# The expert's second bias as a one-row product on TensorE in 22 of 77 visits

## The chip, the cores and the metric

The kernel runs on one core of one Trainium2 chip. The metric is the device time of one execution in microseconds (us). Engines are named as in the profile: PE is TensorE's matmul, PEld its weight load, DVE is VectorE, ACT is ScalarE, POOL is GpSimd and SP is SyncE, which here only starts transfers.

## The reference, cut to what matters

One layer on 32 batches of 256 rows of 128 numbers (8,192 rows): modulated layernorm, attention with 16 heads, a residual sum, and then a mixture of 14 experts of which each row uses one. The change concerns the last part alone:

```python
hid = jnp.einsum('nd,edf->nef', x, w1) + b1          # 128 -> 256
hid = jax.nn.gelu(hid, approximate=False)
all_out = jnp.einsum('nef,efd->ned', hid, w2) + b2   # 256 -> 128, b2: one row of 128 per expert
sel = jnp.take_along_axis(all_out, assignments[:, None, None], axis=1)[:, 0, :]
moe_out = (sel * weights[:, None]).reshape(Bb, Ss, Dd)
...
x = x + gb * moe_out
```

All of it is fp32. `b2` is drawn with a spread of 2, so it matters to the output.

## The kernel before, in words

**Attention stage, 0 to about 491 us.** One batch is one iteration. TensorE makes scores, ScalarE their exponentials, VectorE the row maxima, GpSimd the normalisation and the scatter of finished rows into a table in device memory, sorted by expert. In `project_out` (L1123 to L1133) TensorE already adds a bias by a product of 3 rows (`ones_s` and `bias_rows`, bf16, L1131) ahead of a full one of 128 rows (`w_gated`, fp32, L1132).

**Expert stage, about 491 us to the end.** The table is worked off in NT = 77 *visits* of 128 rows, each with one expert. All engines run the same order of visits, written out by hand; nothing is scheduled by costs. `over_tiles` counts a step j; in step j

- SP has loaded the rows of visit j (`load`, L729 to L746), into one of 21 rooms (16 in `x_s`, 5 in `more_rooms`);
- TensorE (`tile`, L1267) turns visit j (`turn_tile`, L1244: one instruction), makes the first product of visit j-2 (`expand`, L1254: two fp32 matmuls) and the second product of visit j-4 (`contract`, L1263: two fp32 matmuls that add up over the two halves of F in `expert_out`, a PSUM tile with two buffers). In the trace each fp32 matmul of L1254 and L1263 is two records, so such a line shows x4 a visit. Every fourth whole or shared visit, `load_experts` reads four expert numbers into registers (TENSOR_LOAD, at L567) ahead of that step's turn. In step 28 `turn_shared` (L1236, L1237) adds small products. In steps 77 to 80 there is nothing left to turn, and in the last two nothing to expand;
- ScalarE copies the turned rows (L965) and applies gelu to the hidden tile (L972);
- VectorE (`tile`, L2020) copies the next w1 (L1988, where ScalarE doesn't, L987), then for visit n = j-4 adds b2 (`bias_y`, L1993, PSUM to SBUF), finishes visit n-1 with the residual (`out_y`, L2004), multiplies visit n by the gate (`gate_y`, L1998), and for a shared visit merges n-2 into `packed` (L2012). Steps 12 to 25 also hold one piece each of the map of shared visits (L1890 to L1971);
- GpSimd stores finished tiles by indirect DMA (L906, L912).

The waits that matter: `contract(n)` needs `hid_ready` of n and, since `expert_out` has two buffers, `y_biased` of visit n-2 (L1261); VectorE's L1993 needs `y_done` of its visit. A product that waits on `y_biased` holds back every later instruction of TensorE, since the engine works in order. Shared visits begin at 36 and alone make up the last of the 77.

Of the kernel before, what the change touches and what calls it, by code (L numbers as in the profile page):

```python
# [11 lines left out]
ds = bass.ds  # L12

P = 128
D = 128
# [9 lines left out]
FH = F // P  # L25
# [19 lines left out]
H2, X2, GW, ID = 0, D, 2 * D, 3 * D  # L45
# [6 lines left out]
ROOMS = SLOTS + MORE  # L52
NT = T + E - 1
# [16 lines left out]
ACT_HALF = range(16, 32)  # L70

AT_W1, AT_W2, AT_OUT = 2, 4, 5
MAP_TURNED = 8
SHARED_AT = 12
SHARED_TURNED = SHARED_AT + 16
# [16 lines left out]
def need(eng, sem, value):  # L92

    if isinstance(value, int) and value <= 0:
        return
    eng.wait_ge(sem, value)
# [107 lines left out]
def in_range(j):  # L204

    return 0 <= j < NT


def over_tiles(step, begin, lag):

    for j in range(begin, NT + lag):
        step(j, j % SLOTS, j // SLOTS)
# [40 lines left out]
def by_act(q):  # L253

    v = shared_of_visit(q)
    return q < ACT_FIRST or (q in ACT_HALF and q % 2 == 1) or (v is not None and v % 2 == 1)


def fetched(q):

    return sum(1 for k in range(q + 1) if not by_act(k)), sum(1 for k in range(q + 1) if by_act(k))
# [30 lines left out]
def build_adaln_attention_moe(nc, x, w_qkv, b_qk, b_v, w_out, b_out, router_w, w1x, w2, b2, c_t, wmod,  # L292
                              ident, before, expert_row, first_row, tile_numbers, token_numbers, out):
    with ExitStack() as ctx:
        def sb(name, shape, dt=F32):
            return ctx.enter_context(nc.sbuf_tensor(name, shape, dt))
# [4 lines left out]
        def sem(name):  # L301
            return ctx.enter_context(nc.semaphore(name))
# [28 lines left out]
        b2_s = sb("b2_s", [P, E, D])  # L331
# [10 lines left out]
        mod_tmp = sb("mod_tmp", [B, 3, 2 * D])  # L342
        shift_a = sb("shift_a", [P, B])
        scale_a = sb("scale_a", [P, B])
        minus_half = sb("minus_half", [P, 2 * LT])
        eps_s = sb("eps_s", [P, 2 * LT])
        table_first = sb("table_first", [P, 6])
# [80 lines left out]
        rows_in = [x_room[:, s * ROW:s * ROW + ROW] for s in range(SLOTS)]  # L428
# [8 lines left out]
        y_gated_s = sb("y_gated_s", [P, 2, D])  # L437
# [15 lines left out]
        expert_out = [scores[:, 0, m * 512:m * 512 + D] for m in range(2)]  # L453
# [97 lines left out]
        y_done = sem("y_done")  # L551
        y_biased = sem("y_biased")
        y_gated = sem("y_gated")
        out_ready = sem("out_ready")
        out_stored = [sem(f"out_stored{s}") for s in range(SLOTS)]

# [200 lines left out]
        def _(pool):  # L757
# [13 lines left out]
            def root(count):  # L771
                pool.wait_ge(stats, count)
                var = mv[:, :, :, 1:2].rearrange("p k t o -> p (k t o)")
                steps.then(pool.tensor_tensor(rstd[:, 0, :], var, eps_s[:, :], ALU.add))
                pool.tensor_tensor(rstd[:, 1, :], rstd[:, 0, :], minus_half[:, :], ALU.pow).then_inc(rstd_ready, 1)  # L775
# [20 lines left out]
            def attention_rows(b):  # L796

                pool.wait_ge(inverted, b.done())
                need(pool, att_turned, b.n)

                def each_head(v):
                    return v.rearrange("p (n o) -> p n o", o=1).broadcast_to([P, LT * H, DH])

                pool.tensor_tensor(att[:, :, :].rearrange("p t (h d) -> p (t h) d", d=DH), each_head(exp_sum[:, b.slot(2), :]),  # L804
                                   each_head(inverse[:, :]), ALU.mult).then_inc(att_ready, 1)

            def gate(b):

                pool.wait_ge(mod_b_loaded[b.slot(RING_MOD)], 16 * b.earlier(RING_MOD) + 16)
                need(pool, projected, b.n)  # L810
                pool.tensor_tensor(w_gated[:, :], w_out_s[:, :], mod_b[b.slot(RING_MOD)][:, MOD_GA, :], ALU.mult).then_inc(gated, 1)
# [46 lines left out]
            def iteration(b):  # L858
                if b.ago(1).there():
                    attention_rows(b.ago(1))  # L860
                root(b.n + 4)
                if b.ago(2).there():
                    normalise_x2(b.ago(2))
                    modulate2(b.ago(2))
                if b.ago(1).there():
                    gate(b.ago(1))
                if b.ago(-2).there():
                    split_by(pool, steps, b.ago(-2))
                for n in leaving(b):
                    if n >= 0:  # L870
                        weigh_rows(Batch(n))
                if b.ago(-3).there():
                    normalise_x(b.ago(-3))
                if b.n == 0:
                    pool.memset(packed[:, :, :], 0).then_inc(pad_set, 1)
                for s in early_slots(b):
                    pool.wait_ge(rows_loaded[s], 16)
                for n in leaving(b):
                    if n >= 0:
                        scatter(Batch(n), range(1) if n == B - LATE - 1 else range(LT))  # L880
# [177 lines left out]
        def _(pe):  # L1058
# [4 lines left out]
            for n in range(2):  # L1063
                last = pe.matmul(scores[:, 1, n * 512:n * 512 + B], wmod_s[:, n * D:n * D + D], silu, start=True, stop=True)
# [193 lines left out]
            def contract(n):  # L1258
                pe.wait_ge(hid_ready, n + 1)

                need(pe, y_biased, n - 1)  # L1261
                for f in range(FH):
                    last = pe.matmul(expert_out[n % 2], hid[:, n % BUFS, f, :], w2_s[:, ds(expert_of(n), 1), f, :],  # L1263
                                     start=(f == 0), stop=(f == FH - 1))
                last.then_inc(y_done, 1)

            def tile(j, s, turn):  # L1267
                if j == MAP_TURNED:
                    turn_map()
# [60 lines left out]
            over_batches(iteration, drain)  # L1330


            over_tiles(tile, PRIMED, AT_W2)

        @block.vector
        def _(dve):
# [503 lines left out]
            def expert_of(q):  # L1840
                f, v = VISITS[q]
                return whole_experts[f] if v is None else shared_experts[v]
# [147 lines left out]
            def bias_y(n):  # L1990
                k = n % 2
                dve.wait_ge(y_done, n + 1)
                dve.tensor_tensor(y_biased_s[:, k, :], expert_out[k],  # L1993
                                  b2_s[:, ds(expert_of(n), 1), :].rearrange("p o d -> p (o d)"), ALU.add).then_inc(y_biased, 1)

            def gate_y(n):
                dve.wait_ge(y_biased, n + 1)
                dve.tensor_tensor(y_gated_s[:, n % 2, :], y_biased_s[:, n % 2, :], rows_in[n % ROOMS][:, GW:GW + D],  # L1998
                                  ALU.mult).then_inc(y_gated, 1)

            def out_y(n):
                room = rows_in[n % ROOMS]
                dve.wait_ge(y_gated, n + 1)
                dve.tensor_tensor(room[:, GW:GW + D], y_gated_s[:, n % 2, :], room[:, X2:X2 + D], ALU.add).then_inc(out_ready, 1)  # L2004

            def merge(n):
# [6 lines left out]
                                         op0=ALU.bitwise_and, op1=ALU.bitwise_or).then_inc(merged, 1)  # L2013

            def whole_y(n):
                bias_y(n)
                gate_y(n)
                out_y(n)

            def tile(j, s, turn):  # L2020
                if j == SHARED_TURNED + 2:
                    take_shared()
                if whole_reload(j + 1):
                    load_experts(whole_of(j + 1), whole_reload(j + 1))
                if shared_reload(j + 1):
                    load_experts(SHARED_COL + shared_of_visit(j + 1), shared_reload(j + 1))
                if shared_reload(j):
                    load_packed(shared_of_visit(j), shared_reload(j))
                if j == MAP_TURNED - 1:
                    take_map()  # L2030
                n = j - AT_W2
                if shared_of_visit(n) == 0:
                    dve.wait_ge(pad_set, 2)
                if in_range(j + 1) and not by_act(j + 1):
                    fetch_w1(j + 1)
                if n == FIRST + 1:
                    out_y(n)
                elif n == PRIMED:
                    whole_y(n)
                elif n > PRIMED:  # L2040
                    if in_range(n):
                        bias_y(n)
                    if n == NT:
                        merge(n - 2)
                    if n > PRIMED + 1:
                        out_y(n - 1)
                    if in_range(n):
                        gate_y(n)
                    if shared_of_visit(n - 2) is not None and n < NT:
                        merge(n - 2)  # L2050
                steps_shared = (shared_rest, shared_rest_f, shared_places, shared_places_i, shared_split, shared_split_f, shared_spans,
                                shared_before, shared_bounds, shared_low, shared_high, shared_in, shared_columns, shared_edges)
                if 0 <= j - SHARED_AT < len(steps_shared):
                    steps_shared[j - SHARED_AT]()
# [122 lines left out]
```

## Time and profile before

| what | value |
|---|---|
| runs | 603.12, 601.77 and 1474.33 us; median 603.12 |
| the profiled execution | 602.05 us, its span 600.2 us |
| busy share of the span | DVE 92%, ACT 91%, POOL 81%, PE 78%, PEld 44% |
| mean granted TensorE clock | 0.639 |
| chain that ended last | ACT 44%, POOL 17%, PE 15%, DVE 8%, issue 7% |
| instructions | 12121 |

The shares are means over two stages that have different limits: most of ACT's and DVE's busy time lies in the attention stage, which the change leaves alone. The 1474.33 is far off the other two and tells nothing of the kernel. The profiled execution and the other two runs lie within 1.35 us of each other.

### The profile page before, as it was taken

The numbers are of one execution on the slowest core, as the hardware profiler recorded it, in microseconds if no ns is written. First come the engines' busy times: TensorE is split into PE (matmuls) and PEld (weight loads), VectorE is DVE, ScalarE is ACT, GpSimd is POOL, SyncE is SP. The second block draws the span as 40 slices with busy tenths as digits, with TensorE's granted clock in tenths as the row PEclk, the third lists the DMA queues.
The fourth block names the chain that finished last, engine by engine and source line by source line (L and its number), as shares of the span: only waits on it lengthen the run. The fifth ranks groups of instructions, "written<-read, shape, count | busy, mean of one in ns | idle before, by whom it ended". The sixth has DMA issues, their size and how long they took to land.

```text
span 600.2 us, 12121 instructions
## 1 busy us (share of the span) xinstructions
PE 466.0 (78%) x2531; PEld 263.6 (44%) x2531; DVE 550.7 (92%) x1398; ACT 547.8 (91%) x2339; POOL 486.1 (81%) x647
## 2 busy tenths in 40 slices
PE   5456878887887887787787888778777677999993
PEld 2112433443443343343343343334333345889992
DVE  5899999999999999999999999999999977888994
ACT  2599999999999999999999999999999996678881
POOL 4566777989899988999999898999888687777773
PEclk9555565556556556756655655675665558999997
DMA  6366455544555554545455555666555513798760
GB/s 197 105 192 160 136 139 134 142 140 138 144 141 142 142 149 141 150 143 156 148 155 146 151 146 154 172 177 170 153 150 163 157 64 125 231 335 245 236 198 27
DMA packets 77080, 94.42 MB, mean 157 GB/s; under 512 B 12814, under 2 KB 60718, under 8 KB 77006
## 3 DMA queue, kind: packets, MB, share of 16 engines
q1 hardware_dynamic: 68850, 75.69, 45.7%
q0 software_dynamic: 6144, 16.82, 7.5%
q10 hardware_dynamic: 2015, 1.15, 0.8%
q8 instruction: 22, 0.36, 0.3%
q14 instruction: 49, 0.40, 0.2%
HBM read 58.41 MB, written 35.20 MB: 156 GB/s over the span
## 4 chain that ended last, share of the span: by engine, by line
ACT 44%; POOL 17%; PE 15%; DVE 8%; issue 7%; SPq 3%; DMA 3%; ACTq 1%; POOLq 0%; DVEq 0%
ACT scores L940 43%; PE scores L1263 5%; PE scores L1254 5%; POOL table L847 3%; DVE neg_max L1423 3%; SPq L592 3%; POOL xhat L792 2%; POOL rstd L775 2%; PE scores L1244 1%; POOL rest L581 1%; POOL parts L584 1%; POOL h_scaled L815 1%; DMA x_s<-table 1%; POOL att L804 1%; DMA more_rooms<-table 1%
## 5 line engine op out<-in xcount | busy, mean ns | idle before, releaser
L940 ACT ACTIVATE scores<-scores,neg_max 128x256 f32<-128x256 f32 x1024 | 467.2, 808 | 10.8 <-DVE neg_max L1423 10.6
L940 ACT ACTIVATION_READ_ACCUMULATOR scores<-scores,neg_max 128x1 f32 x1024 | 419.8, 569 | 0.0
L1423 DVE TENSOR_REDUCE neg_max<-scores 128x4 f32<-128x1024 f32 x256 | 309.3, 1211 | 7.4 <-PE scores L1104 6.8
L1104 PE MATMUL scores<-k_stack,q_stack 64*128 64x256 bf16 x1024 | 148.2, 388 | 79.6 <-ACT scores L940 65.5
L1104 PEld LDWEIGHTS scores<-k_stack,q_stack 64*128 64x128 bf16 x1024 | 34.1, 106 | 163.5 <-ACT scores L940 116.2
L847 POOL DMA_INDIRECT table<-rows,place_i x64 | 66.1, 1034 | 20.6 <-issue 15.2
L792 POOL TENSOR_SCALAR xhat<-rows,mv,rstd 128x128 f32<-128x128 f32 x60 | 47.6, 794 | 6.8 <-POOL rstd L775 6.8
L1263 PE MATMUL scores<-w_s,hid 128*128 x308 | 49.2, 284 | 1.4 <-DVE y_biased_s L1993 1.2
L1132 PE MATMUL side_a<-w_gated,opt_t 128*128 128x128 f32 x128 | 49.8, 491 | 0.0
L784 POOL TENSOR_SCALAR xhat<-x_s,mv,rstd 128x128 f32<-128x128 f32 x62 | 49.0, 798 | 0.4 <-POOL rstd L775 0.4
L906 POOL DMA_INDIRECT out_dram<-x_s x40 | 39.2, 980 | 12.2 <-issue 8.8
L1263 PEld LDWEIGHTS scores<-w_s,hid 128*128 128x128 f32 x308 | 41.8, 197 | 2.8 <-issue 2.7
L775 POOL TENSOR_TENSOR rstd<-rstd,minus_half 128x4 f32<-128x4 f32 x37 | 38.7, 1045 | 2.9
L972 ACT ACTIVATE hid<-scores,w_ring 128x128 f32<-128x128 f32 x104 | 32.5, 365 | 8.7 <-PE scores L1254 8.2
L581 POOL TENSOR_TENSOR rest<-qk,parts 128x512 f32<-128x512 f32 x31 | 35.8, 1154 | 2.5
L1088 PE MATMUL side_b<-h_t,w_qk_s 128*128 128x256 f32 x62 | 37.3, 705 | 0.6 <-DVE h_t L1409 0.6
L584 POOL TENSOR_TENSOR parts<-rest,parts 128x512 bf16<-128x512 f32 x31 | 35.7, 1153 | 2.5
L1132 PEld LDWEIGHTS side_a<-w_gated,opt_t 128*128 128x128 f32 x128 | 31.3, 303 | 7.3
L1142 PE MATMUL side_b<-ident_s,rows 128*128 128x128 f32 x64 | 18.1, 376 | 19.6 <-POOL rows L816 18.6
L1254 PE MATMUL scores<-x_t,w_ring 128*128 128x128 f32 x208 | 32.8, 281 | 0.0
L1091 PE MATMUL side_b<-h_t,w_qk_s 128*128 128x256 f32 x62 | 32.4, 626 | 0.0
L1149 PEld LDWEIGHTS side_b<-router_s,h_t 128*128 128x128 f32 x128 | 26.7, 273 | 11.1 <-DVE h_t L1447 9.0
(230 smaller groups left out, 882.1 us busy)
## 6 DMA issues: line engine op xcount, KB each, us to landing
q_stack<-parts_dram SPq DMA_DIRECT2D x192, 64.0 KB, 2.9
x_s<-table SPq DMA_DIRECT2D x62, 192.5 KB
parts_dram<-parts SPq DMA_DIRECT2D x31, 384.0 KB
k_stack<-parts_dram SPq DMA_DIRECT2D x186, 64.0 KB, 2.3
mod_b<-mod_rows SPq DMA_DIRECT2D x32, 256.0 KB, 4.4
x_s<-in_x_dram SPq DMA_DIRECT2D x13, 256.0 KB, 5.1
table<-pad_tile SPq DMA_DIRECT2D x15, 192.5 KB
more_rooms<-table SPq DMA_DIRECT2D x15, 192.5 KB
```

What stands on the lines that cost most here:

```text
L581: steps.then(eng.tensor_tensor(rest[:, :, :], qk[:, :, :], parts[:, p, :, 0, :], ALU.subtract))
L584: eng.tensor_tensor(parts[:, p, :, 2, :], rest[:, :, :], parts[:, p, :, 1, :], ALU.subtract).then_inc(parts_ready, 1)
L775: pool.tensor_tensor(rstd[:, 1, :], rstd[:, 0, :], minus_half[:, :], ALU.pow).then_inc(rstd_ready, 1)
L784: last = pool.tensor_scalar(xhat1[b.slot(2)][:, t, :], x_s[:, LT * b.n + t, :], mv[:, 0, t, 0:1], rstd[:, 1, t:t + 1], ALU.subtract, ALU.mult)
L792: last = pool.tensor_scalar(xhat2[:, t, :], rows[b.slot(RING_ROWS)][:, t, X2:X2 + D], mv[:, 1, t, 0:1], rstd[:, 1, LT + t:LT + t + 1], ALU ...
L847: pool.indirect_dma_start(table, bass.IndirectOffsetOnAxis(ap=place_i[g.n % RING_ROWS][:, at.start + t:at.start + t + 1], axis=0), rows[r] ...
L940: last = act.activation(buf[:, k * L:k * L + L], buf[:, k * L:k * L + L], ACT.Exp, bias=neg_max[:, p, n:n + 1], accum_out=exp_sum[:, p, n: ...
L1104: last = pe.matmul(scores[:, c, at:at + L], q_stack[p][r, g + j, t * P:t * P + P], k_stack[p][r, g + j, :], start=True, stop=True)
L1132: last = pe.matmul(to, opt_t[:, t * P:t * P + P], w_gated[:, :], start=False, stop=True, skip_group_check=True)
L1254: last = pe.matmul(hidden[n % 2][:, f * P:f * P + P], w1_e[n % BUFS_W1][:, f * P:f * P + P], x_t[:, n % BUFS, :], start=True, stop=True)
L1263: last = pe.matmul(expert_out[n % 2], hid[:, n % BUFS, f, :], w2_s[:, ds(expert_of(n), 1), f, :], start=(f == 0), stop=(f == FH - 1))
L1423: dve.tensor_reduce(to, scores[:, (PAIRS * b.n + i) % RING, :].rearrange("p (e j m) -> p e j m", e=2, j=2), AX_X, ALU.max, negate=True).th ...
```

## The change

In visits 18 to 30 and 68 to 76 (13 + 9 = 22 visits) `contract` leaves its accumulation open after the second matmul and adds a third, of one row: `ones_row` (1 x 128, all ones) as weights, and the expert's row of `b2_s`, partition 0, as the moving side. Both are fp32. The result in `expert_out` then holds the bias. In these visits VectorE has no `bias_y`; `gate_y` reads `expert_out` itself, after `y_done`, and now gives `y_biased`, which frees the PSUM buffer. `out_y` waits for that. In the other 55 visits nothing changes. GpSimd sets `ones_row` in the first iteration of the attention stage.

```diff
+PE_BIAS = tuple(range(18, 31)) + tuple(range(NT - 9, NT))
...
                 if b.n == 0:
+                    pool.memset(ones_row[:, :], 1.0).then_inc(ones_row_set, 1)
                     pool.memset(packed[:, :, :], 0).then_inc(pad_set, 1)
...
                 need(pe, y_biased, n - 1)
+                adds_bias = bias_by_pe(n)
                 for f in range(FH):
                     last = pe.matmul(expert_out[n % 2], hid[:, n % BUFS, f, :], w2_s[:, ds(expert_of(n), 1), f, :],
-                                     start=(f == 0), stop=(f == FH - 1))
+                                     start=(f == 0), stop=(f == FH - 1 and not adds_bias))
+                if adds_bias:
+                    last = pe.matmul(expert_out[n % 2], ones_row[:, :],
+                                     b2_s[0:1, ds(expert_of(n), 1), :].rearrange("p o d -> p (o d)"), start=False, stop=True)
                 last.then_inc(y_done, 1)
...
             def gate_y(n):
+                if bias_by_pe(n):
+                    dve.wait_ge(y_done, n + 1)
+                    dve.tensor_tensor(y_gated_s[:, n % 2, :], expert_out[n % 2], rows_in[n % ROOMS][:, GW:GW + D],
+                                      ALU.mult).then_inc(y_biased, 1)
+                    return
...
             def out_y(n):
                 room = rows_in[n % ROOMS]
-                dve.wait_ge(y_gated, n + 1)
+                if bias_by_pe(n):
+                    dve.wait_ge(y_biased, n + 1)
+                else:
+                    dve.wait_ge(y_gated, biased_by_dve(n))
...
             def whole_y(n):
-                bias_y(n)
+                if not bias_by_pe(n):
+                    bias_y(n)
...
-                    if in_range(n):
+                    if in_range(n) and not bias_by_pe(n):
                         bias_y(n)
```

The order on TensorE around steps 28 and 29, before (L1263 is the second product, ISA the address made from the expert's number, L567 the register load, L1244 the turn, L1254 the first product, L1236 and L1237 the map's products):

```order
L567 TENSOR_LOAD expert_now
L1244 MATMUL scores<-ident_s,x_s 128x128
L1254 MATMUL scores<-x_t,w1_ring 128x128 x2
L1263 ISA
L1263 MATMUL scores<-w2_s,hid 128x128
L1263 ISA
L1263 MATMUL scores<-w2_s,hid 128x128
L1236 MATMUL side_b<-ident_s,shared_f 1x26 x3
L1237 MATMUL side_b<-edges,ones_s 128x52
```

and with the change (lines 1279 and 1282 are `contract`'s two kinds of product, 1259 the turn, 1269 the first product):

```order
L581 TENSOR_LOAD expert_now
L1259 MATMUL scores<-ident_s,x_s 128x128
L1269 MATMUL scores<-x_t,w1_ring 128x128 x2
L1279 ISA
L1279 MATMUL scores<-w2_s,hid 128x128
L1279 ISA
L1279 MATMUL scores<-w2_s,hid 128x128
L1282 ISA
L1282 MATMUL scores<-b2_s,ones_row 128x128
L1251 MATMUL side_b<-ident_s,shared_f 1x26 x3
L1252 MATMUL side_b<-edges,ones_s 128x52
```

One more address and one more fp32 matmul stand behind each second product; nothing else on TensorE has moved.

The order on VectorE in the last steps, before (L1993 adds b2, L2004 finishes, L1998 gates, L2012 merges):

```order
L1993 ISA
L1993 TENSOR_TENSOR y_biased_s<-scores,b2_s 128x128
L2004 TENSOR_TENSOR x_s<-y_gated_s,x_s 128x128
L1998 TENSOR_TENSOR y_gated_s<-y_biased_s,x_s 128x128
L2012 ISA
L2012 SCALAR_TENSOR_TENSOR packed<-x_s,mine,packed 128x129
```

and with the change (2032 finishes, 2019 gates, 2040 merges):

```order
L2032 TENSOR_TENSOR x_s<-y_gated_s,x_s 128x128
L2019 TENSOR_TENSOR y_gated_s<-scores,x_s 128x128
L2040 ISA
L2040 SCALAR_TENSOR_TENSOR packed<-x_s,mine,packed 128x129
```

The first wait on TensorE's result in a step is now that of the gate, and it stands behind the finishing of the visit before.

## Rows read from the trace of the kernel before

**Rows 1.** The page: granted TensorE clock in 40 slices of 15 us.

```profile
PEclk9555565556556556756655655675665558999997
```

**Rows 2.** Windows: start:end, length, busy us of each engine, clock, DMA, GB/s.

```profile
540.00:550.00 10.00, 10.00 (x90) 9.91 (x90) 9.02 (x42) 8.42 (x33) 7.64 (x8) 1.00 0.88 264
```

**Rows 3.** Timeline of PE, one undisturbed visit: start, length, engine, line, tiles, count.

```profile
563.24 0.27 PE L1244 MATMUL scores<-ident_s,x_s 128*128 128x128 f32 x1
563.35 0.61 PE L1254 MATMUL scores<-x_t,x_s 128*128 128x128 f32 x4
563.79 0.61 PE L1263 MATMUL scores<-w_s,hid 128*128 x4
564.24 0.27 PE L1244 MATMUL scores<-ident_s,x_s 128*128 128x128 f32 x1
```

**Rows 4.** Timeline of PE and PEld, the 3-row product among full ones.

```profile
496.01 0.49 PE L1132 MATMUL side_a<-w_gated,opt_t 128*128 128x128 f32 x2
496.43 0.09 PEld L1131 LDWEIGHTS side_a<-bias_rows,ones_s 3*128 3x128 bf16 x1
496.44 0.22 PE L1131 MATMUL side_a<-bias_rows,ones_s 3*128 3x128 bf16 x1
496.59 0.30 PEld L1132 LDWEIGHTS side_a<-w_gated,opt_t 128*128 128x128 f32 x2
496.59 0.49 PE L1132 MATMUL side_a<-w_gated,opt_t 128*128 128x128 f32 x2
...
496.91 0.38 PE L1142 MATMUL side_b<-ident_s,rows 128*128 128x128 f32 x2
```

**Rows 5.** Timeline of PE, the 26-row products in step 28.

```profile
536.50 0.30 PE L1236 MATMUL side_b<-ident_s,shared_f 26*1 26x26 f32 x6
536.73 0.19 PE L1237 MATMUL side_b<-edges,ones_s 26*128 26x52 bf16 x1
536.86 0.33 PE L1244 MATMUL scores<-ident_s,x_s 128*128 128x128 f32 x1
537.02 0.61 PE L1254 MATMUL scores<-x_t,w_ring 128*128 128x128 f32 x4
```

**Rows 6.** Chain of waits, visits 18 to 30: start, length, engine and line.

```profile
529.64 0.71 PE scores L1263 x4
530.35 0.29 PE scores L1244
530.64 0.61 PE scores L1254 x4
...
534.31 0.71 PE scores L1263 x4
...
535.06 0.30 PE scores L1244
535.37 0.61 PE scores L1254 x4
...
535.98 0.59 PE scores L1263 x4
...
540.23 0.61 PE scores L1254 x4
```

**Rows 7.** Timeline of DVE: the sum that one of these products waits for.

```profile
533.79 0.27 DVE L1993 TENSOR_TENSOR y_biased_s<-scores,b_s 128x128 f32<-128x128 f32 x1
```

**Rows 8.** Chain of waits, TensorE's last visits.

```profile
584.32 0.68 PE scores L1254 x4
...
587.34 0.55 PE scores L1254 x4
```

**Rows 9.** Timeline of DVE, visit 76: its sum and its gate.

```profile
590.41 0.28 DVE L1993 TENSOR_TENSOR y_biased_s<-scores,b_s 128x128 f32<-128x128 f32 x1
...
590.81 0.28 DVE L1998 TENSOR_TENSOR y_gated_s<-y_biased_s,x_s 128x128 f32<-128x128 f32 x1
```

**Rows 10.** Timeline of POOL after the first iteration's memset: brackets are the idle time before.

```profile
42.05 0.45 POOL L811 TENSOR_TENSOR w_gated<-w_out_s,mod_b 128x128 f32<-128x128 f32 x1 [1.24 <-DMA mod_b<-mod_rows]
```

More of the change, by code:

```diff
@@ L72, with bias_by_pe @@
 AT_W1, AT_W2, AT_OUT = 2, 4, 5
+PE_BIAS = tuple(range(18, 31)) + tuple(range(NT - 9, NT))
+def bias_by_pe(q):
+    return q in PE_BIAS
 MAP_TURNED = 8
@@ L256, in by_act, with biased_by_dve @@
     return q < ACT_FIRST or (q in ACT_HALF and q % 2 == 1) or (v is not None and v % 2 == 1)
+def biased_by_dve(q):
+    return sum(1 for k in range(q + 1) if not bias_by_pe(k))
 def fetched(q):
@@ L344, in build_adaln_attention_moe @@
         scale_a = sb("scale_a", [P, B])
+        ones_row = sb("ones_row", [1, P])
         minus_half = sb("minus_half", [P, 2 * LT])
@@ L553, in build_adaln_attention_moe @@
         y_gated = sem("y_gated")
+        ones_row_set = sem("ones_row_set")
         out_ready = sem("out_ready")
@@ L1330, in _ @@
             over_batches(iteration, drain)
+            pe.wait_ge(ones_row_set, 1)
             over_tiles(tile, PRIMED, AT_W2)
```

## Prediction

> **What bounds the kernel now.** I read the page's slices first: the granted clock stands at 5 to 7 tenths through the attention stage and at 9 in the expert stage [rows 1], so I take costs there from rows at full clock. The change touches the attention stage only by a memset of one partition; GpSimd idles 1.24 us for a transfer soon after it [rows 10], which hides it. It would be 0.2 us at most without that cover.
>
> The windows of the expert stage come next. From 540 to 550 us PE is busy 10.00 of 10.00 us and VectorE 9.02 [rows 2]: TensorE is the bound, VectorE close behind. The reader is to see the pace in the timeline: a visit takes 563.24 to 564.24, 1.00 us, of which the turn has 0.11, the first product 0.44 and the second 0.45 [rows 3]. One fp32 matmul is two records at 0.11 each, 0.22 us. A record's modelled end lies behind the start of the next: 563.79 + 0.61 = 564.40, 0.16 after 564.24.
>
> Then the chain of waits shows where TensorE does *not* keep this pace. In the first block of the change, a second product takes 0.71, 0.71 and 0.59 us in place of 0.45 [rows 6]. VectorE was late there: its pieces of the map lie in these steps, and the sum that the one at 534.31 waits for ran from 533.79 to 534.06 [rows 7]. Twice there a register load comes ahead of the turn, which then takes 0.29 and 0.30 us (0.11 is normal), and three first products behind such a load take 0.61 (0.45 is normal), at 530.64, 535.37 and 540.23 [rows 6]. In the last visits VectorE is the bound: TensorE's last visits end, by the pace, well before the sum of visit 76 at 590.41 and its gate at 590.81 [rows 9].
>
> **The change, part by part.** Let c be what one more product costs TensorE where it is the bound.
>
> *The price c.* No row shows a one-row fp32 product. The nearest is the 3-row bf16 one [rows 4]. A full fp32 product starts at 496.01, the 3-row one at 496.44, the next full one at 496.59, and what follows it at 496.91. So the full product that ends in a 3-row one takes 0.43 us instead of 0.22, and the one that is followed by another full-height one takes 0.32. The 0.10 above 0.22 is a weight load that isn't hidden: PEld and PE of the full product both start at 496.59. The remaining 0.11 is a gap at the change of height. The 3-row product itself takes 0.15 (one record). The added one is fp32, two records, so one more 0.11. Together c = 0.11 (gap) + 0.15 + 0.11 (two records) + 0.05 to 0.10 (the next weight load bare; 0.16 instead of 0.11 for the turn behind the 26-row products, 536.86 to 537.02 [rows 5]) = 0.42 to 0.47. I take 0.45, since the row has the same shape of step: full, flat, full. The ends: below, six records of 26 rows and one column of weights take 0.23, 0.04 each [rows 5], so two would be 0.08; above, if each of the two records pays the gap and the bare load, 0.47 + 0.11 = 0.58, call it 0.60.
>
> The Trainium skill speaks against this change at this point: TensorEngine Tiling (Array Packing), "Key Properties", says that a change of tiling mode drains TensorE; the gap in the row agrees with it.
>
> *TensorE pays* 22 x 0.45 = 9.9 us if all of it lies on the path. Between the two blocks, visits 31 to 67, TensorE is the bound and gives nothing back, so a delay made by visit 30 arrives whole at visit 68.
>
> *What the first block gives back.* The waits on VectorE: 0.26 + 0.26 + 0.14 = 0.66 us [rows 6]. VectorE loses a sum of 0.2 us of its pace per visit and TensorE comes 0.45 later, so these waits go. The register loads: they show because TensorE's sequencer stood in such a wait just before; with the array behind its sequencer they should hide, as they do in the undisturbed stretch. Their excess is (0.29 - 0.11) + (0.61 - 0.45) = 0.34 at step 24, (0.30 - 0.11) + 0.16 = 0.35 at step 28, and 0.16 at step 32: 0.85 us. Together 1.51.
>
> *What the last block gives back.* Two first products there take 0.68 and 0.55 us instead of 0.45 [rows 8], 0.33 in all, the first again behind a register load. And VectorE's backlog: from 587.34 + 0.55 = 587.89 three second products follow at 0.45 each, to 589.24, plus 0.16 for the modelled end is 589.40, when visit 76 could have been ready. Its gate ran at 590.81. That 1.41 us falls away, since VectorE's step gets shorter by the sum (sum to gate is 0.40 with the finishing between them [rows 9], so 0.20) while TensorE's second product grows from 0.45 to 0.90. What is late next is TensorE's own last product; VectorE's gate, merges and finishing and GpSimd's last stores stand behind it in the same number and order as before.
>
> *The sum*: 22c - 1.51 - 0.33 - 1.41 = 22c - 3.25. With 0.45 that is 9.9 - 3.25 = **+6.6 us**, so the profiled execution's 602.05 becomes 608.7 us. The median shown is 1.07 above the profiled execution, the other run 0.28 below; I add a third of the distance and say **609.0 us**, 1.0% above 603.12.
>
> Nothing is queued behind a new long wait. VectorE's gate now waits for `y_done` with the merge behind it, but its predecessor waited at the same place. Loads of rows and stores get more time per visit, not less.
>
> **The rivals.**
>
> 1. *A one-row product costs as much as a full one and nothing for the change of height.* c = 0.22: 4.8 - 3.3 = +1.6, and with a shorter delay the register loads hide only in half, so about +2, 604 us. For it: all the 128-column records keep 0.11 [rows 3]. Against it: the 0.43 in [rows 4]. The Trainium skill states this rule in TensorE: Matmul & The Clock Gate, "Why this matters for your kernels": a product of 32 rows takes as long as one of 128. Chance 0.17.
>
> 2. *The other side: faster.* The one-row product slips between its neighbours at the pace of the 26-row records, c = 0.08, no gap. It decides below c = 3.25 / 22 = 0.15. Then TensorE pays 1.8 and gets 3.3 back: -1.5, 600.6 us. For it: 0.23 us for six records [rows 5]. Against it: they have 1 and 26 columns, the added one has 128 and 128, and the gap stands in [rows 4]. Chance 0.06.
>
> 3. *Each record pays.* c = 0.60: 13.2 - 3.3 = +9.9, 612 us. For it: the load of the flat product began with its matmul, 496.43 and 496.44, so nothing ran ahead of it [rows 4]. It also covers a case in which the register loads and the address of the bias don't hide. Chance 0.15.
>
> The forecast keeps 0.62.
>
> **How the numbers follow.** The likeliest case spans c = 0.42 to 0.47, 608 to 609.2 on the profiled execution, and up to 1.1 more by the median. The range has to reach to the cheap rival (604 less the 0.4 by which the other run lies lower) and to most of the dear one: 603.6 to 612.5. It leaves out the faster rival (0.06) and the upper third of the dear one with the tail of unknowns, about 0.1. A measurement of this kernel tells about 2%, 12 us, from no change: slower by that needs 615.2, c of 0.7 or more, 0.05; faster by that isn't reached by any case, 0.01; within it 0.94.
>
> **What would show it.** In the changed profile the step from the start of a second product to the turn behind it should be 0.90 us (0.45 + c) in visits 25 to 30, and a visit 1.45 instead of 1.00; the cheap rival shows 1.22, the dear one 1.60. PEld of the one-row product starts together with its matmul. The second products of the first block no longer wait for VectorE, and the turns behind register loads take 0.11. Visits 31 to 67 keep 1.00. The gate of visit 76 starts 0.1 to 0.2 behind the last one-row record, and the time from it to the end is unchanged. The prediction is wrong if the gap belongs to the change of number type in [rows 4] rather than to the height, or if TensorE's clock leaves its upper level where the one-row products thin its work.

## The result, and the profile after

The change makes the kernel slower: 611.13 us (median; 610.15 to 611.41) against 602.52 us, a ratio of 1.0133 with a 95% interval of 1.0120 to 1.0146, that is +8.0 us (7.2 to 8.8). The medians themselves lie 8.6 us apart; one of the four runs before, 1474.33 us, is far off the others and is left out of the ratio. The change is less than the 2% that the prediction named as what a measurement tells from no change, but the interval is clear of 1. The forecast was 609.0 us in a range of 603.6 to 612.5. The profiled execution took 611.41 us, its span 609.6 us against 600.2.

The pace of TensorE in the first block of the change is the first thing to read. Timeline of PE after the change (start, length, engine, line, tiles, count), step 27, from the turn of visit 27 to that of visit 28; line 1259 is the turn, 1269 the first product, 1279 the second, 1282 the one-row product:

```profile
536.33 0.33 PE L1259 MATMUL scores<-ident_s,x_s 128*128 128x128 f32 x1
536.50 0.61 PE L1269 MATMUL scores<-x_t,w_ring 128*128 128x128 f32 x4
536.94 0.61 PE L1279 MATMUL scores<-w_s,hid 128*128 x4
537.48 0.48 PE L1282 MATMUL scores<-b_s,ones_row 1*128 x2
537.90 0.33 PE L1259 MATMUL scores<-ident_s,x_s 128*128 128x128 f32 x1
```

A visit takes 537.90 - 536.33 = 1.57 us where [rows 3] had 1.00. The second product lasts 0.54 instead of 0.45 until the next starts, the one-row product 0.42, and the turn 0.17 instead of 0.11. So the added product costs 0.57 us: 0.09 ahead of it, 0.42 itself and 0.06 behind it. The weight loads of the same place show where it goes (timeline of PEld):

```profile
536.83 0.53 PEld L1279 LDWEIGHTS scores<-w_s,hid 128*128 128x128 f32 x4
537.48 0.29 PEld L1282 LDWEIGHTS scores<-b_s,ones_row 1*128 1x128 f32 x2
537.89 0.14 PEld L1259 LDWEIGHTS scores<-ident_s,x_s 128*128 128x128 f32 x1
```

The load for the second product starts 0.11 before its matmul (536.83, 536.94); the one for the flat product starts with it (537.48 in both), and so does the turn's (537.89, 537.90). This answers to [rows 4], where the 3-row product showed the same.

The register loads all but vanish: the chain of waits over steps 24 and 28 in the changed profile has 0.26 for the turn, as in every step of the block, and 0.49 and 0.45 for the first product, where [rows 6] had 0.61 for both. (The chain counts from modelled end to modelled end, so its 0.26 is not the 0.17 of the timeline.)

```profile
531.65 0.26 PE scores L1259
531.91 0.49 PE scores L1269 x4
...
537.97 0.26 PE scores L1259
538.23 0.45 PE scores L1269 x4
```

Behind the first block the pace is the old one, 549.22 + 0.06 for the last turn behind a flat product and then 1.00:

```profile
550.28 0.27 PE L1259 MATMUL scores<-ident_s,x_s 128*128 128x128 f32 x1
...
551.28 0.27 PE L1259 MATMUL scores<-ident_s,more_rooms 128*128 128x128 f32 x1
```

At the end VectorE now waits for TensorE. Timeline of both, visits 75 and 76 (line 2019 is the gate, of 75 at 599.07 and of 76 at 600.13; PE's lines are the two kinds of product of visit 76; brackets hold the idle time before and what ended it), answering to [rows 9]:

```profile
598.96 0.71 PE L1279 MATMUL scores<-w_s,hid 128*128 x4
599.07 0.29 DVE L2019 TENSOR_TENSOR y_gated_s<-scores,x_s 128x128 f32<-128x128 f32 x1 [0.30 <-PE scores L1282]
599.61 0.48 PE L1282 MATMUL scores<-b_s,ones_row 1*128 x2
600.13 0.29 DVE L2019 TENSOR_TENSOR y_gated_s<-scores,x_s 128x128 f32<-128x128 f32 x1 [0.30 <-PE scores L1282]
```

The windows show who has time to spare in the first block; the first is of the change, the second of before (start:end, length, busy us of PE, PEld, DVE, ACT, POOL, clock, DMA, GB/s):

```profile
530.00:548.00 18.00, 18.00 (x132) 15.24 (x132) 10.82 (x56) 11.26 (x38) 13.78 (x14) 1.00 0.85 270
```

```profile
528.00:543.00 15.00, 14.90 (x122) 13.53 (x121) 13.70 (x74) 11.89 (x44) 11.34 (x13) 1.00 0.94 307
```

VectorE falls from 91% busy to 60%, TensorE from 99% to 100%. The work was taken off the engine that had nearly enough time and put on the one that had none. The clock is at its upper level (1.00, 2.4 GHz) in both.

Four starts cut the stage into stretches that can be compared between executions: the turns of visits 22, 35 and 72, and the gate of visit 76 (before: 527.67, 543.13, 581.00 and 590.81; after: 528.30, 549.22, 587.13 and 600.13). All later runs are in the same table; each cell is a difference of two starts in the timeline, in us.

| kernel | 22 to 35 | 35 to 72 | 72 to gate 76 | sum |
|---|---|---|---|---|
| before | 15.46 | 37.87 | 9.81 | 63.14 |
| the change | 20.92 | 37.91 | 13.00 | 71.83 |
| e2 full height, fp32 | 17.33 | 38.01 | 10.07 | 65.41 |
| e3 first block alone | 20.92 | 38.15 | 9.91 | 68.98 |
| e4 last block alone | 15.76 | 37.83 | 13.00 | 66.59 |
| e5 no sum, no product | 15.25 | 38.09 | 8.83 | 62.17 |
| e6 full height, bf16 parts | 15.46 | 38.33 | 9.26 | 63.05 |
| e7 the same, 14 visits | 15.51 | 38.21 | 9.06 | 62.78 |

The change adds 5.46 + 0.04 + 3.19 = 8.69 us. Of the rest of the span's 9.4, 0.63 lies ahead of the turn of visit 22, which differs more than that between executions in which nothing ahead of it differs but GpSimd's memsets (527.67 before, 527.13 in e1, 530.04 in e4).

Each cell comes from one execution, so a difference is worth no more than the spread of unchanged stretches. The stretch 22 to 35 is unchanged in e1 and e4 as well and took 16.18 and 15.76 us there against 15.46 before: 0.7 of spread. The stretch from 72 to the gate is unchanged in e1 and e3, with 10.06 and 9.91 against 9.81: 0.25. In e1 most of the first comes from one place, the register load ahead of the turn in step 28 (see e5): from the turn of 27 to that of 28 it is 2.09 us there and 1.51 before.

### The profile page after: what moved, and what is told of

Same layout as the page of the kernel before. It is cut to its first block, busy times and chain, and to the rows that moved or that the text cites. A ratio compares the mean times of both kernels' runs of the same rounds, so it can differ in the third digit from the quotient of the medians.

```text
span 609.6 us, 12188 instructions
## 1 busy us (share of the span) xinstructions
PE 481.3 (79%) x2575; PEld 272.5 (45%) x2575; DVE 548.9 (90%) x1376; ACT 548.8 (90%) x2339; POOL 486.1 (80%) x648
## 4 chain that ended last, share of the span: by engine, by line
ACT 43%; POOL 19%; PE 16%; DVE 8%; issue 7%; DMA 3%; SPq 2%; ACTq 1%; POOLq 0%; DVEq 0%
ACT scores L955 43%; PE scores L1279 5%; PE scores L1269 5%; DVE neg_max L1443 3%; POOL table L861 3%; POOL xhat L806 3%; POOL rstd L789 2%; POOL rest L595 2%; POOL parts L598 2%; PE scores L1259 2%; PE scores L1282 1%; POOL h_scaled L829 1%; SPq L606 1%; POOL att L818 1%; POOL xhat L798 1%
## 5 line engine op out<-in xcount | busy, mean ns | idle before, releaser
L955 ACT ACTIVATION_READ_ACCUMULATOR scores<-scores,neg_max 128x1 f32 x1024 | 437.9, 602 | 0.0
L1119 PE MATMUL scores<-k_stack,q_stack 64*128 64x256 bf16 x1024 | 149.9, 391 | 75.2 <-ACT scores L955 65.3
```

Source lines behind the costliest of these rows:

```text
L955: last = act.activation(buf[:, k * L:k * L + L], buf[:, k * L:k * L + L], ACT.Exp, bias=neg_max[:, p, n:n + 1], accum_out=exp_sum[:, p, n: ...
L1119: last = pe.matmul(scores[:, c, at:at + L], q_stack[p][r, g + j, t * P:t * P + P], k_stack[p][r, g + j, :], start=True, stop=True)
```

## The experiments

**e1: the price by itself.** The kernel before, with products of zeros in visits 40 to 63, so that nothing else changes:

```diff
+            def zeros_of(n):
+                kinds = ([(zero_f, 1)], [(zero_b, 1)], [(zero_f, P)], [(zero_b, P)], [(zero_f, 64)], [(zero_f, 1)] * 2)
+                return kinds[(n - 40) // 4] if 40 <= n < 64 else []
...
+                for k, (zero, rows_) in enumerate(more):
+                    last = pe.matmul(expert_out[n % 2], zero[0:rows_, :], zero[0:rows_, :], start=False, stop=(k == len(more) - 1))
```

> The kernel before, with extra products of zeros added to the second product in the stretch where TensorE alone sets the pace (1.00 us a visit): visits 40-43 one row fp32, 44-47 one row bf16, 48-51 128 rows fp32, 52-55 128 rows bf16, 56-59 64 rows fp32, 60-63 two one-row fp32 products one after the other. Theory A (price = gap at a change of height + the flat product's own serial records + a bare weight load behind): a visit takes 1.57, 1.31 (a 0.15 record), 1.23 (no gap, two records of 0.11), 1.06 to 1.11, about 1.5, and 1.98 (the gap and the bare load once, 0.41 twice). Theory B (the price belongs to the fp32 number type or to the address made from a register, not to the height): 128 rows fp32 costs the same 0.57 as one row, so 1.57, and one row bf16 at most 1.11. Theory C (every third product costs the same because the accumulation is longer): all single ones alike.

e1 was run once; its clock stands at 1.00 from 540 to 590 us. Timeline of PE in e1: each kind once, with the turn behind it and for three of them the turn ahead, so that the visit can be read, as 555.60 - 554.03 = 1.57 (line 1273 is the second product, 1276 the zeros, 1249 the turn).

```profile
554.03 0.33 PE L1249 MATMUL scores<-ident_s,x_s 128*128 128x128 f32 x1
...
555.18 0.48 PE L1276 MATMUL scores<-zero_f 1*128 1x128 f32 x2
555.60 0.33 PE L1249 MATMUL scores<-ident_s,x_s 128*128 128x128 f32 x1
...
561.20 0.22 PE L1276 MATMUL scores<-zero_b 1*128 1x128 bf16 x1
561.35 0.33 PE L1249 MATMUL scores<-ident_s,x_s 128*128 128x128 f32 x1
...
566.48 0.27 PE L1249 MATMUL scores<-ident_s,x_s 128*128 128x128 f32 x1
...
567.48 0.39 PE L1276 MATMUL scores<-zero_f 128*128 128x128 f32 x2
567.71 0.27 PE L1249 MATMUL scores<-ident_s,x_s 128*128 128x128 f32 x1
...
573.20 0.22 PE L1276 MATMUL scores<-zero_b 128*128 128x128 bf16 x1
573.25 0.28 PE L1249 MATMUL scores<-ident_s,more_rooms 128*128 128x128 f32 x1
...
575.93 0.49 PE L1276 MATMUL scores<-zero_f 64*128 64x128 f32 x2
576.34 0.33 PE L1249 MATMUL scores<-ident_s,more_rooms 128*128 128x128 f32 x1
...
583.06 0.33 PE L1249 MATMUL scores<-ident_s,x_s 128*128 128x128 f32 x1
...
584.22 0.71 PE L1276 MATMUL scores<-zero_f 1*128 1x128 f32 x4
584.85 0.33 PE L1249 MATMUL scores<-ident_s,x_s 128*128 128x128 f32 x1
```

| extra product | visit, turn to turn | price |
|---|---|---|
| 1 row, fp32 | 1.57 | 0.57 |
| 1 row, bf16 | 1.31 | 0.31 |
| 128 rows, fp32 | 1.22 | 0.22 |
| 128 rows, bf16 | 1.06 | 0.06 |
| 64 rows, fp32 | 1.57 | 0.57 |
| two of 1 row, fp32 | 1.79 | 0.79 |

It is the height. In the same number type 1 and 64 rows cost the same 0.57 and 128 rows 0.22; theories B and C fall, and since these zeros have a fixed address and cost the 0.57 that the change's product costs, the address from a register adds nothing. One expectation missed: two flat products cost 0.79, not 0.98. The second adds only 0.22, the price of a full one. So each record does not pay for the height; the *switch* does, once: 0.09 of gap, the first weight load bare, the next bare again. The gap belongs to the height and not to the number type, a case in which the prediction called itself wrong: the second product lasts 0.54 until a flat one starts in either type, and 0.44 or 0.45 until a full one does. Between flat and full the whole switch is 0.57 - 0.22 = 0.35 us in fp32 and 0.31 - 0.06 = 0.25 in bf16. An estimate from the loads accounts for the difference: one-row loads take 182 to 184 ns in fp32 and 90 ns in bf16 in these traces. 0.18 + 2 x 0.11 = 0.40 is near the 0.42 of the flat fp32 product, 0.09 + 0.06 the 0.15 of the bf16 one, and 0.18 + 4 x 0.11 = 0.62 the 0.63 of the pair. Why a change of height leaves the gap and bares the loads, these runs don't show.

**e2: the same product at full height.**

```diff
-        ones_row = sb("ones_row", [1, P])
+        first_ones = sb("first_ones", [P, P])
...
+                    pool.memset(first_ones[:, :], 0.0).then_inc(ones_row_set, 1)
+                    pool.wait_ge(ones_row_set, 1)
+                    pool.memset(first_ones[0:1, :], 1.0).then_inc(ones_row_set, 1)
...
-                    last = pe.matmul(expert_out[n % 2], ones_row[:, :],
-                                     b2_s[0:1, ds(expert_of(n), 1), :].rearrange("p o d -> p (o d)"), start=False, stop=True)
+                    last = pe.matmul(expert_out[n % 2], first_ones[:, :],
+                                     b2_s[:, ds(expert_of(n), 1), :].rearrange("p o d -> p (o d)"), start=False, stop=True)
```

> The change with the ones row padded by zeros to 128 rows and b2 read on all 128 partitions, so the third product has the height of its neighbours. Theory A: c = 0.22 in place of 0.565, first block paces 1.23 a visit; 22c = 4.9 less 3.2 to 3.9 given back = +1.0 to +1.7 us against before (603.5 to 604.2), 7 us faster than the change. Theory B: no different from the change, 611.

Measured: a ratio of 1.0024 (0.9991 to 1.0057) to before, +1.4 us, as theory A expected (1.0 to 1.7), and not told from no change; theory B's 611 us falls. The undisturbed steps of the first block run at 1.23 a visit. This adds 127 rows of work per product and takes off most of the loss: 2.27 us added between the four starts instead of 8.69.

**e3 and e4: each block alone.** One line each:

```diff
-PE_BIAS = tuple(range(18, 31)) + tuple(range(NT - 9, NT))
+PE_BIAS = tuple(range(18, 31))            # e3
+PE_BIAS = tuple(range(NT - 9, NT))        # e4
```

> The change in visits 18 to 30 alone. The two traces give +5.5 us between the turn of visit 22 and that of visit 35. Theory A (a delay made there is passed on whole, since TensorE sets the pace to the end): +5.5 us against before. Rival (VectorE's backlog in the last visits absorbs part): since the backlog forms only after the last visits speed up, it should absorb nothing; if it does, +4 or less.

> The change in visits 68 to 76 alone. The two traces give +3.2 us between the turn of visit 72 and the gate of visit 76. Theory A (the blocks add): +3.2 us against before, and this and the first block alone sum to the whole change's +8.6. Rival (they interact): the sum is off by over 1 us.

Measured: e3 1.0079 (1.0058 to 1.0101), +4.8 us (3.5 to 6.1); e4 1.0035 (1.0015 to 1.0056), +2.1 us (0.9 to 3.4). Both intervals hold what was expected (5.5 and 3.2). The sum, 6.9, is 1.7 under the expected 8.6 and 1.1 under the change's 8.0. That is over the 1 us that the rival of interacting blocks was to show, but intervals of over 1 us on either side of each term allow it, so the times decide nothing here. The traces do: e3's first stretch and e4's last are those of the change to the hundredth (20.92 and 13.00), and the stretch between moves by 0.04 in the change and by 0.28 in e3 (at most 0.46 in any kernel of the table). So a delay made by visit 30 is passed on, and the blocks add.

**e5: neither sum nor product.** In the 22 visits b2 is not added at all. This shows what is given back when c is 0:

```diff
-                adds_bias = bias_by_pe(n)
+                adds_bias = False
```

> In the 22 visits of the change VectorE's sum is left out and no third product is put in, so b2 is missing there (this part of the computation is left out). It shows what is given back with c = 0. By the account of the prediction at most 3.25 us; with no added product to hide behind, the register loads of steps 24, 28 and 32 (0.85) hide only in part and the wait of step 23 on visit 17's sum (0.26) stays, so -2.1 to -3.2 us against before. Rival (VectorE's sums never held TensorE up in a way that reaches the end): 0, not over -0.7.

Measured: 0.9975 (0.9961 to 0.9989), -1.5 us (-2.4 to -0.7). The rival of no gain (not over 0.7) is all but ruled out, and the gain is below the expected 2.1 to 3.2, whose weak end the interval just reaches. The table says where: 0.98 us at the end, only 0.21 in the first block (0.2 to 0.9, going by the three unchanged executions). There the wait on visit 17's sum stays, as expected, and the register loads do not hide; two turns still start late. Timeline of PE in e5, steps 24 and 28 (line 1279 is the second product, 1259 the turn):

```profile
530.67 0.30 PE L1259 MATMUL scores<-ident_s,x_s 128*128 128x128 f32 x1 [0.20 <-issue]
...
534.43 0.61 PE L1279 MATMUL scores<-w_s,hid 128*128 x4
535.38 0.30 PE L1259 MATMUL scores<-ident_s,x_s 128*128 128x128 f32 x1 [0.34 <-issue]
```

The second of them (step 28) starts 0.95 us after its second product did, where 0.45 is the pace; before it was 535.06 - 534.31 = 0.75 [rows 6]. The same step takes 0.93 in e4 and 1.29 in e1, where this block is unchanged, so the 0.95 is within the spread of executions. But in those the product itself started late, 0.65 to 0.69 behind its first product, and here it didn't (533.98 to 534.43, 0.45). So the late turn doesn't need a wait on VectorE's sum just before, which is what the prediction put it down to. What holds the register load was not tried.

**e6 and e7: the cheap form.** By e1's table the cheapest product that adds b2 is a full-height bf16 one. b2 is split once into three bf16 rows that add up to it, and the weights have three rows of ones:

```diff
+                if b.n == 2:
...
+                    steps.then(pool.tensor_copy(b2_out[:, 0, :], b2_rows[:, 0, :]))
+                    steps.then(pool.tensor_tensor(b2_rows[:, 1, :], b2_rows[:, 0, :], b2_out[:, 0, :], ALU.subtract))
+                    steps.then(pool.tensor_copy(b2_out[:, 1, :], b2_rows[:, 1, :]))
+                    pool.tensor_tensor(b2_out[:, 2, :], b2_rows[:, 1, :], b2_out[:, 1, :], ALU.subtract).then_inc(ones_row_set, 1)
...
+                    last = pe.matmul(expert_out[n % 2], three_ones[:, :],
+                                     b2_of[:, ds(expert_of(n), 1), :].rearrange("p o d -> p (o d)"), start=False, stop=True)
...
+PE_BIAS = tuple(range(16, 25)) + tuple(range(NT - 5, NT))     # e7; e6 keeps the 22 visits
```

The parts lie in the first three partitions of the score stage's `q_stack[0]`, which is free by then; what is left in the other partitions is multiplied by zero.

> The change in the same 22 visits, with b2 split once into three bf16 rows that add up to it, and the third product of full height in bf16 (weights: three rows of ones, the rest zero; one record). By the prices measured before c = 0.06 instead of 0.565: 22 x 0.06 = 1.4 less 2.1 to 3.9 given back = -0.7 to -2.5 us against before, 10 us faster than the change. Rival (the setup, some small work of GpSimd in iteration 2 and a transfer after batch 30, reaches the critical chain): at or above before.

> The same product only where VectorE was late: visits 16 to 24 and the last five (14 instead of 22). 14 x 0.06 = 0.9 less the same 2.1 to 3.9, so about 0.5 us faster than the 22-visit version, -1.2 to -3.0 us against before. Rival (the last block needs all nine visits for VectorE to catch up): slower than the 22-visit version by 0.5 or more.

Measured: e6 0.9989 (0.9976 to 1.0001), -0.7 us; e7 0.9984 (0.9971 to 0.9997), -1.0 us (-1.8 to -0.2). e6 lies at the weak end of what was expected (-0.7), with an interval that reaches no change; e7 just misses its own (-1.2), with an interval that reaches into it. The two can't be told from each other, and e7's rival, slower than e6 by 0.5 or more, did not show. In the timeline of e6, step 28 (line 1307 is the product with the parts, 1282 the turn), the product costs 0.06 and the turn is not held up by the register load:

```profile
535.50 0.22 PE L1307 MATMUL scores<-q_stack,three_ones 128*128 x1
535.56 0.28 PE L1282 MATMUL scores<-ident_s,x_s 128*128 128x128 f32 x1
```

In step 24 of the same trace it still is; the turn starts 0.33 behind the product:

```profile
530.78 0.22 PE L1307 MATMUL scores<-q_stack,three_ones 128*128 x1
531.11 0.30 PE L1282 MATMUL scores<-ident_s,x_s 128*128 128x128 f32 x1
```

e7 is the one version with the full result whose interval lies below the kernel before, by 0.03 to 0.29%. At one interval in several that close to 1, this is a hint of a gain and no more.

## Why the prediction was right, and where its sizes were off

**TensorE sets the pace and nothing is given back between the blocks: right.** 37.91 against 37.87 us, and e3.

**The price c: the mechanism right, the size too small.** The forecast took 0.45 us; measured are 0.57 with a turn behind it and 0.61 with another product behind it (visits 72 to 75, whose next product then takes 0.64 instead of 0.45 in the chain). Visit 76 has nothing behind it and pays 0.09 + 0.42 = 0.51. The step that was mis-sized is "0.15 + 0.11 (two records)". The 0.15 of [rows 4] was a bf16 record, and most of it is a weight load in the open (0.09); the fp32 load takes 0.18, and each of two fp32 records streams 0.11. That makes 0.40 by this estimate and 0.42 as measured, in place of 0.26. The gap, 0.11 in the forecast, is 0.09, the bare load behind it 0.06 as said. In all 17 x 0.57 + 4 x 0.61 + 0.51 = 12.6 us instead of 9.9.

By the prediction's own sign the dear rival was the nearer one. A visit was to take 1.45 us by the forecast and 1.60 by the dear rival, and it takes 1.57; the time, 611.13 us, is also nearer to that rival's 612 than to 609.0. The dear rival named nearly the right price (0.60) with the wrong reason, that each record pays for the height; e1's pair shows that it doesn't. The cheap rival is refuted by e1: a one-row product does not cost what a full one does when its neighbours are full. The Trainium skill's rule on which it stood (TensorE: Matmul & The Clock Gate, "Why this matters for your kernels") is for one product by itself, which no run here shows. The rule that spoke against the change (TensorEngine Tiling (Array Packing), "Key Properties": a change of tiling mode drains TensorE) agrees with the gap and the two bare loads, 0.35 us for the whole switch in fp32 (0.57 less 0.22); that a lower product counts as such a change is not shown. The faster rival needed c under 0.15, which only the full-height bf16 product has; e6's -0.7 us lies on that side, but its interval reaches no change.

**What is given back: near in size, less well explained.** Forecast 3.25 us, by the traces 12.6 - 8.7 = 3.9 us: 13 x 0.57 - 5.46 = 1.9 in the first block (forecast 1.51) and 2.0 in the last (1.74). Two parts of the working don't hold.

The first is the list of waits. One more second product of the first block was late behind VectorE than the three of the sum, in step 22. Its sum runs from 527.85 to 528.12, and the product starts 0.25 behind, at 528.37, as the one at 534.31 did behind its sum [rows 7]. Leaving it out did no harm, since it isn't given back. Chain of waits, the second product of step 22, before and after the change:

```profile
528.39 0.68 PE scores L1263 x4
```

```profile
529.02 0.65 PE scores L1279 x4
```

The second is that the register loads show because of a wait just before. In e5 the one in step 28 shows without any such wait. And what is given back seems to be no constant. With c of 0, 0.06, 0.22 and 0.57 the first block gives back 0.2, 0.8, 1.0 and 1.9 us, the last 1.0, 1.1, 1.7 and 2.0 (from the table, the price of its 13 or 9 products less the difference to before). With 0.7 and 0.25 us of spread between executions, smaller steps in these rows can't be told from none; the ends of each row can be told apart. This suggests that a good part of it isn't VectorE's time saved but TensorE's own delay covering gaps that any slower product would cover; no run has the slower product with VectorE's sum kept in these visits, so it is not shown. The forecast's formula 22c - 3.25 was right near the c it was worked out for; at c = 0 it says -3.25, and -1.5 (-2.4 to -0.7) was measured.

**The end.** The gate of 76 was said to follow the last one-row record by 0.1 to 0.2. It starts 0.04 after that record's modelled end (599.61 + 0.48 = 600.09), so TensorE's last product did come to be what is late, as said. From the gate to the end of the span it is 9.5 us against 9.4, unchanged as said.

In the traces the forecast's +6.6 us becomes 8.7 by two errors, +2.7 by the price and -0.7 by what is given back. That the second takes off a part of the first is luck. The time stayed inside the range because the range reached to most of the dear rival.

## What to carry to other kernels

Ask who sets the pace before moving an operation off a busy engine: 90% busy with the other at 100% is the engine that can keep the work. A bias as a matmul was cheap here only at the height of its neighbours, where its weight load hides, and cheapest in bf16, so pad it to that height; a product with 128 times the rows was cheaper by 0.35 us each. Even so the best version gained 0.16%, not clearly more than nothing. When a price is read from a row of another number type, split the row into weight load and stream before scaling it, and don't count a gap as given back before a run shows what holds it open.

## What the runs showed of the hardware that was not expected

- The price of a change of height does not depend on how flat the product is (1 and 64 rows alike, 0.57 us), and two flat products in a row pay it once (0.79 us).
- A full-height bf16 product of 128 columns among fp32 ones costs TensorE 0.06 us, a tenth of the one-row fp32 product.
- VectorE's gate reads PSUM in 0.28 to 0.29 us, as it read SBUF in 0.28 before [rows 9].
